# A three-part layer kernel: two more weight matrices scaled by their whole norm, scales made as powers on GpSimd, the first product begun with the upper halves, and a new order of the prologue and of four passes

## What is computed

```python
def ffn(x, A, B, Wr):                  # A: 64 x 16 x 512, B: 64 x 512 x 16, Wr: 64 x 512
    scores = x @ Wr.T
    top_vals, top_idx = top_k(scores, 16)
    G = zeros(N, 64); G[rows, top_idx] = softmax(top_vals)
    h = einsum('nd,krd->nkr', x, A)
    return 2.0 * einsum('nkr,kdr->nd', h * G[:, :, None], B)

def attn(x, w_gate, w_up, w_down):     # 1376 x 512, 1376 x 512, 512 x 1376
    s = silu(x @ w_gate.T)
    s[the 688 entries of the row with the smallest |s|] = 0
    return (s * (x @ w_up.T)) @ w_down.T

x = x + 0.5 * ffn(norm(x)); x = x + attn(norm(x)); x = x + 0.5 * ffn(norm(x))
```

## Time and profile before

| what | value |
|---|---|
| median of 3 runs | 715.1 us (714.95 to 715.6) |
| the profiled execution | 715.56 us |
| its span in the profile | 713.7 us |
| TensorE matmul busy | 695.4 us, 97% |
| VectorE busy | 474.7 us, 67% |
| ScalarE busy | 360.8 us, 51% |
| GpSimd busy | 201.7 us, 28% |
| granted TensorE clock | 1.00 of full |

### The profile page before, as it was taken

The page is one execution under the profiler, slowest core; times in us unless marked ns, Lnnn a source line. Parts: engine busy times, 40 slices in busy tenths (PEclk is TensorE's granted clock), DMA queues, the critical chain, the costliest instruction groups (busy, mean ns, idle before and its releaser), DMA issues.

```text
span 713.7 us, 10326 instructions
## 1 busy us (share of the span) xinstructions
PE 695.4 (97%) x3683; PEld 332.1 (47%) x3683; DVE 474.7 (67%) x1004; ACT 360.8 (51%) x458; POOL 201.7 (28%) x526
## 2 busy tenths in 40 slices
PE   5999999999999999999999999999999999899997
PEld 2444444545444444444445444444544444444443
DVE  4999688658586666747666575566647575638862
ACT  5867985545635254453535545253452526576220
POOL 1110334332314142240523315142331424344000
PEclk9999999999999999999999999999999999999999
DMA  9866234151734172341514334252432324123442
GB/s 332 271 166 171 75 60 86 27 102 39 137 51 95 36 109 60 85 89 41 104 30 101 74 69 88 48 89 42 98 61 51 65 44 86 31 56 71 86 89 73
DMA packets 171722, 62.27 MB, mean 87 GB/s; under 512 B 163632, under 2 KB 163632, under 8 KB 171664
## 3 DMA queue, kind: packets, MB, share of 16 engines
q1 hardware_dynamic: 171664, 61.56, 39.4%
HBM read 16.97 MB, written 4.19 MB: 30 GB/s over the span
## 4 chain that ended last, share of the span: by engine, by line
PE 80%; DVE 5%; ACT 5%; POOL 4%; issue 3%; DMA 2%; SPq 0%; DVEq 0%; POOLq 0%; ACTq 0%
PE ps L564 16%; PE ps L566 16%; PE ps L565 16%; PE ps L658 11%; PE ps L662 11%; PE ps L659 11%; ACT signs L856 3%; POOL small L493 2%; DMA mem<-w_a 1%; POOL small L490 1%; POOL small L489 1%; DVE mem L1174 1%; PE ps L585 1%; DVE w_a_lo L1079 1%; POOL small L491 1%
## 5 line engine op out<-in xcount | busy, mean ns | idle before, releaser
L856 ACT ACTIVATE signs<-mem,small 128x1376 bf16<-128x1376 f32 x112 | 161.3, 1441 | 143.2 <-POOL small L493 128.3
L658 PE MATMUL ps<-w_b_hi,pt_hi 128*128 128x512 f16 x256 | 97.0, 379 | 1.6 <-DVE x L1161 1.0
L564 PE MATMUL ps<-w_a_hi,xt_f 128*128 128x512 f16 x256 | 97.0, 379 | 1.1 <-DVE w_a_lo L1079 1.1
L659 PE MATMUL ps<-w_b_lo,pt_hi 128*128 128x512 f16 x256 | 97.0, 379 | 0.0
L566 PE MATMUL ps<-w_a_lo,xt_f 128*128 128x512 f16 x256 | 97.0, 379 | 0.0
L565 PE MATMUL ps<-w_a_hi,xt_f 128*128 128x512 f16 x256 | 97.0, 379 | 0.0
L564 PE MATMUL ps<-w_u_hi,xt 128*128 128x512 f16 (+1 forms) x192 | 68.5, 357 | 0.4 <-DVE mem L1174 0.4
L489 POOL TENSOR_SCALAR small<-small 128x1 f32<-128x1 f32 x96 | 28.4, 296 | 142.9 <-ACT signs L856 142.1
L564 PE MATMUL ps<-w_g_hi,xt 128*128 128x512 f16 (+1 forms) x192 | 68.5, 357 | 0.2 <-DVE mem L1181 0.2
L565 PE MATMUL ps<-w_g_hi,xt 128*128 128x512 f16 (+1 forms) x192 | 68.5, 357 | 0.0
L566 PE MATMUL ps<-w_g_lo,xt 128*128 128x512 f16 (+1 forms) x192 | 68.5, 357 | 0.0
(11 more groups left out here) (138 smaller groups left out, 1197.9 us busy)
## 6 DMA issues: line engine op xcount, KB each, us to landing
x<-x SPq DMA_DIRECT2D x14, 256.0 KB, 3.7
out<-x SPq DMA_DIRECT2D x14, 256.0 KB, 2.3
mem<-w_g SPq DMA_DIRECT2D x4, 688.0 KB, 12.5
mem<-w_u SPq DMA_DIRECT2D x4, 688.0 KB, 4.8
mem<-w_d SPq DMA_DIRECT2D x5, 512.0 KB, 4.7
mem<-w_a SPq DMA_DIRECT2D x4, 512.0 KB, 6.9
mem<-w_b SPq DMA_DIRECT2D x4, 512.0 KB, 9.2
pt_hi<-p_hi SPq DMA_TRANSPOSE x32, 3.2
```

The lines of the kernel that those rows point to most:

```text
L564: pe.matmul(dst, x_hi, w_hi, start=start, stop=False)
L658: pe.matmul(dst, x_hi[:, c, :], hi[m.name][:, c, :], start=c == 0, stop=False)
L659: pe.matmul(dst, x_hi[:, c, :], lo[m.name][:, c, :], start=False, stop=False)
L856: act.activation(signs[:, :], mags[h], ACT.Sign, bias=thr[h], scale=-1.0, accum_out=bal[h]).then_inc(counted[h], 1)
```

## The change

- `w_a` and `w_u` join `WHOLE`. Their norms are one-column matmuls on the row sums of the squares. Each piece of `w_a` is squared in two halves: ScalarE takes the left 512 columns, VectorE the right ones (`square_right`), so its norm has two one-column matmuls for each piece. The norm of `w_u` goes to bank 2.
- VectorE only reads a norm (`read_norm`). GpSimd makes the scale as (norm / 2^30) to the power -1/2 (`make_scale`), and products of scales (`make_inverse`), whose reciprocals VectorE takes (`make_unscale`). The scales are no longer powers of two. The squares of `w_d` lie in `signs` and `keep` in turn.
- The statistics of sublayer 1 have two buffers. Reading the scores is taken out of `choose` for the first six calls (`read_scores`).
- The first call of w_a runs in the order of `experts_begun`: upper-half products of a quarter need only `split_hi`, the products with the lower half follow one quarter later, and the transposes of tile 1 stand behind the second quarter's upper products; sixteen fillers stand ahead of it.
- combine 1 writes bank `DOWN`, and combine 2 waits only for the first `add_ffn`.
- Each engine's list is in a new order in the prologue, in passes 0 to 2, and in tile(1), which now has the order of the other tiles. The gates of tile 2 start when two banks of tile 1's ups have been read.

The core of the diff:

```diff
@@ build
-    WHOLE = [MR, MB, MD]
+    WHOLE = [MR, MA, MB, MU, MD]
@@ comb_bank
-            return bank(WIDE if k == len(calls) - 2 else COMB)
+            return bank({1: DOWN, len(calls) - 2: WIDE}.get(k, COMB))
@@ gpsimd
+            def make_scale(m):
+                pool.wait_ge(norm_ready, MATS.index(m) + 1)
+                link(pool.tensor_scalar(norm_part[m.name], norm2[m.name], 2.0 ** -30, 2.0 ** -120,
+                                        ALU.mult, ALU.max))
+                pool.tensor_tensor(scale[m.name], norm_part[m.name], neg_half[:, :], ALU.pow
+                                   ).then_inc(scale_made, 1)
+            def make_inverse(names, by):
...
@@ tensor
+            def experts_begun(e, x_hi, x_lo, turn_of):
+                for c in range(DC + 1):
+                    for o in range(2):
+                        dst, cols = bank(e + o), slice(o * BANK, (o + 1) * BANK)
+                        if c < DC:
+                            pe.wait_ge(w_hi_made, pieces_before(MA) + c + 1)
+                            pe.matmul(dst, x_hi[c], hi["a"][:, c, cols], start=c == 0, stop=False)
+                            pe.matmul(dst, x_lo[c], hi["a"][:, c, cols], start=False, stop=False)
+                    if c == 1:
+                        turn(turn_of)
+                    for o in range(2):
+                        dst, cols = bank(e + o), slice(o * BANK, (o + 1) * BANK)
+                        if c:
+                            wait_low(pe, MA, c - 1)
+                            mm = pe.matmul(dst, x_hi[c - 1], lo["a"][:, c - 1, cols], start=False,
+                                           stop=c == DC)
+                return mm
...
-                    busy(12)
-                    turn(turn_of)
...
-                    busy(4)
-                    for c in range(DC):
-                        split_done(MA, c)
-                        for o in range(2):
-                            mm = three(bank(e + o), MA, c, slice(o * BANK, (o + 1) * BANK),
-                                       x_hi[c], x_lo[c], c == 0, c == DC - 1)
+                    busy(16)
+                    mm = experts_begun(e, x_hi, x_lo, turn_of)
...
             experts(1, 3)
+            combine(1, 0, fresh=True)
             norms(MG)
-            combine(1, 0, fresh=True)
             combine(1, 1)
             pe.wait_ge(scale_made, 4)
             norms(MU)
             experts(1, 4)
+            combine(1, 2)
             pe.wait_ge(routed_ready, LEAD - 1)
+            pe.wait_ge(scale_made, 5)
             gates(0, fresh=True)
-            combine(1, 2)
+            combine(1, 3)
+            norms(MD)
             ups(0, fresh=True)
-            combine(1, 3)
-            pe.wait_ge(scale_made, 5)
-            gates(1, norms_of=MD)
             combine(1, 4)
+            gates(1)
+            experts(1, LEAD)
             pe.wait_ge(scale_made, 6)
             ups(1, flags_of=0)
-            experts(1, LEAD)
+            gates(2)
             down(0, fresh=True)
-            gates(2)
             combine(1, LEAD)
@@ scalar
+            x_to_hi(2, 1)
+            exps(4)
+            for n in range(len(MD.pieces)):
+                square(MD, n)
             tanh(0)
-            x_to_hi(2, 1)
-            square(MD, 0)
-            square(MD, 1)
+            p_to_hi(4)
             magnitude(0)
+            x_to_hi(2, 2)
+            act.wait_ge(squared, pieces_before(MD) + len(MD.pieces))
             count(0, 0)
...
-            count(2, 0)
+            act.wait_ge(counted[1], ROUNDS)
+            counts(2, 0, 1, 2)
             v_to_hi(1)
@@ vector
+            read_norm(MA)
             norm_stats(1, 1)
-            make_scale(MA)
+            read_scores(0)
+            norm_stats(1, 2)
+            split_lo(MA, 0)
             norm_apply(1, 1)
-            split_lo(MA, 0)
             split_lo(MA, 1)
-            norm_stats(1, 2)
             split_lo(MA, 2)
+            norm_apply(1, 2)
+            split_lo(MA, 3)
             turned_to_lo(1)
...
@@ sync
             load_x(1)
+            load_x(2)
             load_w(MB, 0, 1, 2, 3)
-            load_x(2)
```

More of the change, by code:

```diff
@@ L269, in sum_at, with right_sum_at @@
             return sum(len(k.pieces) for k in WHOLE[:WHOLE.index(m)]) + n
+        def right_sum_at(n):
+            return sum(len(k.pieces) for k in WHOLE) + n
         def staged(m, c, n, rows):
@@ L575, in norms @@
                     if m in WHOLE:
+                        last = n == len(m.pieces) - 1
                         top = 2 * sum_at(m, n) + 1
-                        pe.matmul(bank(m.bank, 1), ones[0:rows, :],
-                                  square_tops[0:rows, top:top + 1], start=n == 0,
-                                  stop=n == len(m.pieces) - 1).then_inc(norm_summed, 1)
+                        mm = pe.matmul(bank(m.bank, 1), ones[0:rows, :],
+                                       square_tops[0:rows, top:top + 1], start=n == 0,
+                                       stop=last and m is not MA)
+                        if m is MA:
+                            pe.wait_ge(a_right_squared, n + 1)
+                            top = 2 * right_sum_at(n) + 1
+                            mm = pe.matmul(bank(m.bank, 1), ones[:, :], square_tops[:, top:top + 1],
+                                           start=False, stop=last)
+                        mm.then_inc(norm_summed, 1)
                         continue
@@ L701, in gates @@
                 pe.wait_ge(xt_loaded[2], 16 * (t + 1))
-                last = t == NT - 1
-                if last:
-                    pe.wait_ge(val_begun, 1)
+                early = t in (2, NT - 1)
+                if early:
+                    pe.wait_ge(val_begun, 1 if t == 2 else 2)
                 elif t:
                     pe.wait_ge(val_ready, t)
-                wide(MG, t, fresh, norms_of=norms_of, behind=t if last else None
+                wide(MG, t, fresh, norms_of=norms_of, behind=t if early else None
                      ).then_inc(gate_done, 1)
@@ L809, in square @@
                 act.wait_ge(w_loaded[m.name][n], 16)
-                if m is MD and n == 0:
-                    wait_low(act, MU, len(MU.pieces) - 1)
-                if m in WHOLE:
+                if m is MD and n >= 2:
+                    act.wait_ge(squared, pieces_before(m) + n - 1)
+                if m is MA:
+                    at = sum_at(m, n)
+                    act.activation(squares(m, n)[:, 0:BANK], staged(m, c, k, rows)[:, 0, 0:BANK],
+                                   ACT.Square, accum_out=square_sums[:, at:at + 1]
+                                   ).then_inc(squared, 1)
+                elif m in WHOLE:
                     at = sum_at(m, n)
@@ new lines, in read_norm, with make_unscale, square_right @@
+                op.then_inc(norm_ready, 1)
+            def make_unscale(dst, names):
+                dve.wait_ge(inverse_made, list(inverse).index(names) + 1)
+                link(dve.reciprocal(dst, inverse[names]))
+            def square_right(n):
+                c, k, rows = MA.pieces[n]
+                half = staged(MA, c, k, rows)[:, 0, BANK:KR]
+                at = right_sum_at(n)
+                dve.wait_ge(w_loaded["a"][n], 16)
+                dve.scalar_tensor_tensor(out=squares(MA, n)[:, BANK:KR], in0=half, scalar=1.0,
+                                         in1=half, op0=ALU.mult, op1=ALU.mult,
+                                         accum_out=square_sums[:, at:at + 1]
+                                         ).then_inc(a_right_squared, 1)
```

363 lines of the change are left out of this document (181 added, 182 removed).

## The result

The changed kernel takes 717.6 us, the median of seven runs from 717.28 to 718.71, beside 714.95 us for the kernel before on the same chip. The ratio is 1.0041, with a 95% interval from 1.0029 to 1.0053: slower by 2.1 to 3.8 us where the prediction had 6.2 us in favour. The profiled execution took 717.54 us with a span of 715.8 us, 2.1 us above the span before.

The account below looks back on a forecast made before the run. The prediction took TensorE, busy for 695.4 of 713.7 us, as the bound. Gains of 3.8, 1.0 and 1.7 us less 0.3 us made 6.2 us: 715.1 to 708.9 us, range 706.6 to 711.9 us.

Parts of the forecast that it names:

- rival C: Prologue: tanh(0) queued behind six w_d squares delays silu(0), ups(0) and tile 0's counts; 717.6 us at 9 us; chance 0.04.
- Part 1: Norm of w_u on TensorE: one-column matmuls replace twelve column sums and a wait of 1.39 us; gain 3.8 us.
- Part 2: combine(1, 1) in bank DOWN no longer waits for add_ffn(1, 0): gain 1.0 us; combine(1, 0) costs 0, at worst 1.
- Part 3: First call of w_a: A's scale and splits come sooner, the second call starts earlier; gain 1.7 us.
- Part 4: VectorE and GpSimd keep up with TensorE 6.5 us ahead at ups(0), margin about one microsecond; cost 0.3 us.
- Rival A: VectorE becomes the bound of the prologue, giving back 1.5 to 5 us, most likely 3: 711.9 us; chance 0.26.
- Part 5: Reordered passes 0 to 2 and tile(1): w_d squares ahead of tanh(0) cost nothing; down(1) costs 0, at worst 2.
- The tightest spot is `down(1)`: Upper half of down(1), margin 0.8 us: needed by 134.5 us, made at 133.9 us; cost 0, at worst 2.
- the first part: What bounds the kernel: TensorE never waits between 58 and 616 us, so time won before 58 us reaches the end.
- a sign of being wrong: A gap on TensorE ahead of ups(0) or down(1), released by VectorE or a transpose, would show the forecast wrong.

Follow-up runs that it names:

- e1_tanh: The changed kernel with tanh(0) ahead of the last three of the six w_d squares on ScalarE: 714.99 us, 1.0004 of the kernel before.
- e4_vhi: e3_both with v_to_hi(0) and v_to_hi(1) one count earlier on ScalarE: 710.52 us, 0.9943 of the kernel before.
- e2_nolock: The changed kernel with three VectorE waits, so that three w_d splits start only after tile 0's search of that moment: 714.6 us, 1.0002 of the kernel before.
- e7_pool_vhi: e1_tanh with GpSimd's w_d scale between tile 0's searches, splits one count later and guarded, v_to_hi(0) and v_to_hi(1) one count earlier: 710.57 us.
- e3_both: The changed kernel with the edits of e1_tanh and e2_nolock together: 712.13 us, 0.9963 of the kernel before.
- e5_fill: The changed kernel with 40 unread 128-column matmuls between the norm of w_d and ups(0) on TensorE: 718.37 us, 1.005 of the kernel before.
- p1_mu: The kernel before with only w_u's norm changed, to four one-column matmuls behind experts(1, 4): 715.52 us, 1.0006 of the kernel before.

## Why the prediction was wrong

**The sign and the number.** 717.6 us lies outside the range, on the side that had a chance of 0.04. It is also, to the digit, the number given for rival C, and the mechanism of C was at work; but the agreement is chance. C priced a `silu(0)` 9 us late. It ended at 75.70 us, 1.2 us after the 74.5 us at which the prediction had it due, and by C's own rule ("It turns the sign once `silu(0)` ends 6.5 us after 74.5 us") that would have left the kernel faster. e1_tanh gives C's cause 2.6 us. What made up the rest is the second cause, and what let either of them matter is the chain behind them. From 717.6 us down to the 708.9 us forecast, the squares account for 2.6 us, the searches beside the splits for 3.0 us and the place of `v_to_hi` for 1.6 us; the last 1.6 us are what e4_vhi still lacks (see below).

**Part 1** (3.8 us): in the trace as predicted, the norm of `w_u` takes 0.1 us at 50.1 us without a wait. **Part 2** (1.0 us): right, combine(1, 1) follows at 44.90 us without a gap, and combine(1, 0) meets none either at 37.40 us.

**Part 3** (1.7 us): the direction was right and the size was off, 3.3 us. The first `w_a_hi` split came at 12.70 us, not 13.35: the halves were squared by 11.3 us, and GpSimd's scale took 1.0 us from the copy, where 0.9 was forecast. The larger error was the clock. I let it double at 16.9 us; here the 512-column matmuls were 0.22 us apart from 14.61 us, and the call ended at 20.33 us, held by VectorE's last split, 0.6 us before the 20.9 us that the prediction gave for a fast clock. That moment is not fixed. In five of the ten profiled executions with this first call (e2_nolock and e4_vhi to e7_pool_vhi) the last slow matmul started between 16.1 and 17.4 us, around the 16.9 us of the prediction; over the ten executions the second call began between 19.99 and 21.75 us, a gain of 1.9 to 3.6 us.

**Part 4** (cost 0.3 us): the ledger held. VectorE was through with everything ahead of `silu(0)` at 70.98 us; with 1.59 us for it, that is 72.6 us, where the prediction said 73.3. Rival A was not needed: VectorE did not become the bound, it waited for ScalarE. Of GpSimd's scales, `w_d`'s took 1.7 us, with its products 2.9. That size was forecast (2 us). But count(0, 1), which the prediction names behind it, was weighed by `gated(0)` alone, not as a link of the seven: the 2.7 us more between the first two counts had no term, and in e3_both and e4_vhi 2.3 us of them are still there (counts 5.4 us apart).

**Part 5** is the step that failed, in two places. The first is "Six `w_d` squares (1.1 us each) now stand ahead of `tanh(0)`: by my walk they run from 63 to 69.3 us ... No cost". They ran from 62.29 to 72.69 us. The first came when it should; the walk had the other five right behind it, and three of them waited for their loads. SyncE in order of time:

```profile
58.18 1.09 SPq L320 DMA_DIRECT2D mem<-w_d  x2
59.32 1.23 SPq L368 DMA_TRANSPOSE pt_lo<-p_lo  x1
60.59 3.04 SPq L320 DMA_DIRECT2D mem<-w_d  x4
```

The six loads share the queue with transposes, the last four are issued over 3 us, and from issue to landing they took 4.1 to 9.2 us, with a median of 7.3 us (4.0 to 6.9 and 4.7 us before).

The second is "The tightest spot is `down(1)`". There was a tighter one, `down(0)`, with 0.5 us (108.72 us and the landing time of the earlier trace rows, against 112.81 us). And the walk to `down(1)` took counts 3 us apart, their spacing in the kernel before. Where splits of `w_d` alternate with counts, they were 4.05 us apart.

Both rest on an inference of the first part: TensorE has no gap between 58 and 616 us, hence "Whatever is won or lost before 58 us is therefore carried to the end, unless the change makes a new gap". Winning time by itself makes new gaps where another chain is close. A missing gap says that nothing was later than TensorE, not by how much. Another chain stood 0.5 us behind it. To carry 6.2 us forward, each operand of the passes after it had to come 6.2 us sooner too. Theory 2 was this, and e1_tanh, e2_nolock, e3_both and the first part of e5_fill bear it out; p1_mu shows the same with other operands, the `w_g` splits. The prediction had named a gap ahead of `ups(0)` or `down(1)` as a sign of being wrong, and both came.

The rule that the prediction drew from the Trainium skill (SBUF - State Buffer, "SBUF: two separate sides") applied after all, at a place where I had not looked for it: there it was weighed for GpSimd's scales, and it acted on the searches. It says that a VectorE operation with two SBUF inputs and a GpSimd one that reads SBUF exclude one another for a whole instruction. The rows agree: 0.34 us became 1.41 us when both started at 93.89 us, and e2_nolock gives 3.0 us back by keeping them apart.

**What stays open.** e4_vhi is 4.3 us faster than before, not the 6.2 us of the sum. In the nine executions with the narrow norm of `w_u`, the norm of `w_d` began between 73.04 and 74.11 us, so that TensorE was 6.6 to 7.7 us ahead at that point; e4_vhi, at 73.97 us, was 6.7 us ahead, and its three remaining gaps hold 2.1 us. That leaves 0.3 us, less than the runs can tell. What moves this point by 1.1 us between executions (the clock's rise, and a wait for `xt_f` near 27 us of 0 to 1.6 us) was not taken apart. Why the loads landed late (the transposes between them, or the other traffic) was not tried. They still matter in e4_vhi: the chain that ended last, followed back, runs from VectorE's `w_g` split at 58.06 us, which frees the room for the load, through a load of `w_d` that landed at 71.84 us, 9.1 us after its issue, to the last squares and the first count at 76.32 us. That is only 0.6 us before its place in the kernel before (76.93 us), although combine(1, 3), the work behind `gates(0)`, began 1.9 us sooner (68.80 for 70.65 us, there combine(1, 2)). No run moved all six squares, or their loads.

## What to carry to other kernels

A bound engine without a gap does not show how close the next chain is: before you carry a gain forward, walk each operand of the next stages (here a transpose 0.5 us ahead of its reader) and see whether it comes earlier too. When you put bulk work of one engine ahead of or beside a latency chain, price it by what it waits for and by what it locks out, since here three meetings with an instruction of 0.34 us cost 3.0 us, half of what the change was to save. And where a chain is the bound, an added wait that keeps a large VectorE operation away from it can make the kernel faster.

## What the runs showed of the hardware

- A GpSimd operation on one element in each partition took 0.34 us alone and 1.34 to 1.79 us beside a VectorE operation with two SBUF inputs (1.28 or 1.65 us long). Keeping three such meetings apart was worth 3.0 us of 717.6.
- Three profiled executions had a stretch of nine 512-column matmuls at 1.2 GHz, most of them 0.43 us apart and 1.7 us longer in all than at 2.4 GHz: at once behind a gap of 2.42 us in the changed kernel, 0.65 us after a gap of 3.44 us in e5_fill, and 0.4 us after the second of two gaps of 1.52 and 0.76 us in p1_mu. After the 2.79 us in e1_tanh and the 1.75 us in e2_nolock there was none, nor behind the gap that e5_fill filled. A stall can thus cost more than its own length, and its length alone does not say whether it does.
- Six plain loads of 192 to 512 KB issued among transposes took 4.1 to 9.2 us to land.
